# Attention scores with the head matrix folded into 33 key features instead of into the queries, and 3 of 16 probability tiles multiplied by the values in fp32

## What is computed

```python
c_q = h_t @ W_DQ + b_DQ                      # 32 query latents a token
c_kv = h_t @ W_DKV + b_DKV                   # 32 key/value latents a token
q_c, k_c, v_c = c_q @ W_UQ + b_UQ, c_kv @ W_UK + b_UK, c_kv @ W_UV + b_UV   # 8 heads of 128
q_r = c_q @ W_QR + b_QR                      # 8 heads of 32
k_r = h_t @ W_KR + b_KR                      # 32, the same for all heads
scores = einsum('bhsd,bhtd->bhst', concat(q_c, q_r), concat(k_c, k_r)) * scale
o = einsum('bhst,bhtd->bhsd', softmax(scores), v_c)
```

## Time and profile before

| | us |
|---|---|
| median of three runs | 1004.38 |
| profiled execution | 1002.61 |
| its span, first to last instruction | 1000.9 |
| first stage | 0 to 86 |
| attention, from its first PE instruction | 86 to 604 |
| the two later stages | 605 to 1000.9 |

### The profile page before, as it was taken

The page is one execution under the profiler, slowest core; times in us unless marked ns, Lnnn a source line. Parts: engine busy times, 40 slices in busy tenths (PEclk is TensorE's granted clock), DMA queues, the critical chain, the costliest instruction groups (busy, mean ns, idle before and its releaser), DMA issues. The chain is left out here.

```text
span 1000.9 us, 21467 instructions
## 1 busy us (share of the span) xinstructions
PE 881.8 (88%) x8406; PEld 527.7 (53%) x8406; DVE 713.9 (71%) x1315; ACT 588.0 (59%) x1004; POOL 655.7 (66%) x437
## 2 busy tenths in 40 slices
PE   4893899999999999999999988962499999999995
PEld 1350244444444444444444547862266777677764
DVE  4768888888888888888898836872075666566643
ACT  3750577777777777777777663664265446544650
POOL 4200599999999999999999993698404524442452
PEclk9995799999999999999999998985599999999998
DMA  9910000000000000000000004259525434543110
GB/s 279 339 43 0 1 2 2 2 2 2 2 2 2 2 2 2 2 2 2 2 2 1 3 1 169 99 198 320 201 69 162 143 107 140 175 142 123 43 52 19
DMA packets 48166, 71.61 MB, mean 72 GB/s; under 512 B 7508, under 2 KB 40473, under 8 KB 47938
## 3 DMA queue, kind: packets, MB, share of 16 engines
q1 hardware_dynamic: 38114, 53.13, 16.1%
q0 software_dynamic: 7680, 16.87, 5.2%
q10 hardware_dynamic: 2272, 0.24, 0.2%
HBM read 46.76 MB, written 29.67 MB: 76 GB/s over the span
## 5 line engine op out<-in xcount | busy, mean ns | idle before, releaser
L834 POOL TENSOR_TENSOR prob_lo<-prob 128x1024 f16<-128x1024 f32 x208 | 437.3, 2130 | 95.0 <-ACT prob L799 94.9
L799 ACT ACTIVATE prob<-st_ps 128x512 f32<-128x512 f32 x512 | 301.4, 597 | 131.8 <-PE st_ps L723 129.5
L859 DVE TENSOR_REDUCE part_max<-x_ps 128x1 f32<-128x512 f32 x512 | 325.1, 678 | 66.7 <-PE x_ps L733 65.7
L722 PE MATMUL st_ps<-QA,KA 128*128 128x512 f16 x512 | 198.1, 387 | 0.5 <-ACT prob L799 0.5
L723 PE MATMUL st_ps<-QB,KB 65*128 65x512 f16 x512 | 196.4, 384 | 0.0
L771 PE MATMUL acc_ps<-VV,prob 128*128 128x65 f16 x2048 | 159.3, 194 | 3.9 <-POOL prob_lo L834 3.9
L771 PEld LDWEIGHTS acc_ps<-VV,prob 128*128 128x128 bf16 x2048 | 143.6, 98 | 33.4 <-POOL prob_lo L834 6.1
L771 PE MATMUL acc_ps<-VV,prob_lo 128*128 128x65 f16 x2048 | 158.7, 194 | 0.0
L771 PEld LDWEIGHTS acc_ps<-VV,prob_lo 128*128 128x128 f16 x2048 | 134.9, 98 | 29.9
L1340 POOL DMA_INDIRECT out<-yo,xb x48 | 47.7, 993 | 153.3 <-DVE yo L1447 151.1
L732 PE MATMUL x_ps<-KA,QA 64*128 64x512 f16 x256 | 102.2, 399 | 20.8 <-DVE part_max L859 20.7
(11 more groups left out here) (177 smaller groups left out, 1346.7 us busy)
## 6 DMA issues: line engine op xcount, KB each, us to landing
w1f<-in_L_ffn_w SPq DMA_DIRECT2D x8, 1024.0 KB, 6.1
w2f<-in_L_ffn_w SPq DMA_DIRECT2D x8, 1024.0 KB, 6.1
xbuf<-zeros SPq DMA_DIRECT2D x7, 910.0 KB, 16.7
xb<-xbuf SPq DMA_DIRECT2D x8, 780.0 KB, 5.4
x<-in_L_attn_h_t SPq DMA_DIRECT2D x8, 512.0 KB, 8.9
out<-x SPq DMA_DIRECT2D x4, 1024.0 KB, 5.9
tbuf<-x SPq DMA_DIRECT2D x4, 1024.0 KB, 9.7
tbuf<-gb_row SPq DMA_DIRECT2D x4, 1024.0 KB, 4.7
```

The source lines that it names most:

```text
L722: mm(st_ps[i % 2][:], KA[:, at], QA[:, n % QRING, half], start=True, stop=False)
L799: nc.scalar.activation(prob[:, k, f * HALF:(f + 1) * HALF], st_ps[i % 2][:], ACT.Exp).then_inc(exp_done, 1)
L834: nc.gpsimd.tensor_tensor(prob_lo[:, k, :], prob[:, k, :], prob_top[:, k, :], ALU.subtract).then_inc(sub_pool, 1)
L859: nc.vector.tensor_reduce(part_max[:, n % 2, item // 2, item % 2:item % 2 + 1], x_ps[i % 3][:], AX.X, ALU.max).then_inc(smax_done, 1)
```

## The change

1. **The matrix goes into the keys.** `keys(n, f)` makes, from KA and a copy KB of its high rows, 98 rows of key features (33 numbers high, 32 and 33 more for the low parts) with two products, GH (128 rows) and GL (64 rows). ACT copies all 98 rows to KX, a ring of three heads; DVE then replaces rows 64 to 96 by the low part (`keys_low`). CQ is used as it is by all heads; it is there twice (parity of the head), for the sake of one row more, the maximum's. The second copy is made by a DMA at the start of the stage.
2. **A score half is one product** of 99 rows, KX against CQ.
3. **Maxima by 512 columns.** For every 128 queries there are two products of 98 rows, CQ against one half of KX; each is issued by itself when one of three x_ps buffers is free, one behind each score half. The 128 queries of a product are every eighth one, so mz lies in such an order that a DMA can write it into the row of CQ directly: `max_rows` on PE and ACT falls away. Before the first maxima product of a head PE waits for both halves of `keys_low` (kl_done).
4. **Whole tiles.** Tiles 1 and 6 of even heads and tile 3 of odd ones aren't split: PE multiplies prob (fp32) with V32, the values in fp32, 33 columns, 8 products a tile. DVE subtracts no tile any more; POOL subtracts 13 of 16 as before.
5. In the first stage, KC is no longer made, V32 is made by DVE (one addition a batch), and the folded matrix is made in two steps of four heads (`FOLD`) in place of one.

```diff
-        def maxima_of(p, k):
...
+                def scores(n, k, f):
...
+                    if k == 0 and f == 0:
                         te.wait_ge(mrow_in[n % 2], 16 * (n // 2 + 1))
-                    mm(st_ps[i % 2][:], KA[:, at], QA[:, n % QRING, half], start=True, stop=False)
-                    mm(st_ps[i % 2][:], KB[:, at], QB[:, n % QRING, half], start=False, stop=True).then_inc(scores_ready, 1)
+                    mm(st_ps[i % 2][:], KX[:, n % KRING, k * P:(k + 1) * P],
+                       CQ[:, n % 2, b * S + f * HALF:b * S + (f + 1) * HALF], start=True, stop=True).then_inc(scores_ready, 1)
...
-                    mm(x_ps[i % 3][:], QA[0:LR, n % QRING, at], KA[0:LR, b * S:b * S + HALF], start=True, stop=True)
-                    mm(x_ps[(i + 1) % 3][:], QA[LR:P, n % QRING, at], KC[LR:P, b, :], start=True, stop=True).then_inc(smax_ready, 1)
+                def maxima(n, j, f):
+                    i = (n * ST + j) * 2 + f
+                    if i >= 3:
+                        te.wait_ge(smax_done, i - 2)
+                    if j == 0 and f == 0:
+                        te.wait_ge(kl_done, 2 * n + 2)
+                        if n == 1:
+                            te.wait_ge(copied, 16)
+                    mm(x_ps[i % 3][:], queries_of[:, n % 2, b * P:(b + 1) * P, j],
+                       KX[0:QROWS, n % KRING, f * HALF:(f + 1) * HALF], start=True, stop=True).then_inc(smax_ready, 1)
...
+                def keys(n, f):
+                    if 2 * n + f:
+                        te.wait_ge(kl_done, 2 * n + f)
+                    mm(side_ps[0:QROWS, :], GH[:, h, :], KA[:, at], start=True, stop=False)
+                    mm(side_ps[0:QROWS, :], GL[:, h, :], KB[:, at], start=False, stop=True).then_inc(k_ready, 1)
...
+                    if k in whole(n):
+                        te.wait_ge(exp_done, (n * ST + k) * 2 + 2)
+                        for q in range(ST):
+                            last = mm(acc_ps[:, q, DC:VC], prob[:, k, q * P:(q + 1) * P], V32[:, b * ST + k, :],
+                                      start=False, stop=False)
...
+                def keys_low(n, f):
+                    v.wait_ge(kh_done, 2 * n + f + 1)
+                    at = KX[LR:QROWS - 1, n % KRING, f * HALF:(f + 1) * HALF]
+                    nc.vector.tensor_tensor(at, side_ps[LR:QROWS - 1, :], at, ALU.subtract).then_inc(kl_done, 1)
...
+                    if is_head(p + 2):
+                        maxima(p + 2, k, 1)
+                        if k == ST - 1:
+                            whole_rows(p + 2)
+                    if k - 1 in KEY_SLOTS and is_head(p + 3):
+                        keys_low(p + 3, KEY_SLOTS.index(k - 1))
```

More of the change, by code:

```diff
@@ L142, in adaln_block @@
         ukvT = sb(one, "ukvT", [P, H, 2 * DC])
-        G = sb(one, "G", [QROWS, H, P])
+        G = sb(one, "G", [P, H, QROWS])
         zeros = sb(one, "zeros", [P, 7, ROW])
@@ L344, in _ @@
                 pool.wait_ge(ln_rstd, 2)
-                fill(13, CQ[3 * DC:QROWS, :], 1.0)
+                fill(13, CQ[3 * DC:QROWS, 0, :], 1.0)
                 pool.wait_ge(const_p, 14)
-                for g in range(2, NG):
+                power(2)
+                pool.wait_ge(ln_rstd, 3)
+                fill(14, V32[:, :, DC:DC + 1], 1.0)
+                pool.wait_ge(const_p, 15)
+                for g in range(3, NG):
                     power(g)
@@ L498, in _ @@
                 queries_low(2)
-                side_out(GQS)
+                side_out(FOLD)
+                side_out(FOLD + 1)
                 take_values(2)
@@ L572, in side @@
                                                        ident[0:2 * DC, 0:2 * DC])
-                    elif n == GQS:
-                        for h in range(H):
-                            last = mm(bank[0:QROWS, h * DC:(h + 1) * DC], uqT[:, h, 0:QROWS], ukvT[:, h, 0:DC], start=True, stop=True)
+                    elif n >= FOLD:
+                        for i in range(4):
+                            h = 4 * (n - FOLD) + i
+                            at = slice(i * P, i * P + QROWS)
+                            for r in (0, LR):
+                                mm(bank[r:r + DC, at], ukvT[:, h, 0:DC], uqT[:, h, 0:QROWS], start=True, stop=True)
+                                last = mm(bank[r + DC:r + LR, at], qr[:, h, :], ident[0:QROWS, 0:QROWS], start=True, stop=True)
                     elif n < BIAS:
@@ L615, in _ @@
                 latent(2, 1)
-                side(GQS)
+                side(FOLD)
                 turn(7)
+                side(FOLD + 1)
                 values(2)
@@ L663, in adaln_block, with whole @@
         AHEAD = 4
-        QUERY_SLOTS = (4, 6)
-        FIRST_MAX = 0
-        ROW_SLOT = 1
-        def by_vector(n):
-            return (5, 7) if n % 2 else (5,)
+        KEY_SLOTS = (4, 6)
+        queries_of = CQ[0:QROWS, :, :].rearrange("c r (g t) -> c r g t", t=ST)
+        def whole(n):
+            return (3,) if n % 2 else (1, 6)
         def by_pool(n):
-            return [k for k in range(ST) if k not in by_vector(n)]
+            return [k for k in range(ST) if k not in whole(n)]
         pool_before = [sum(len(by_pool(m)) for m in range(n)) for n in range(HEADS)]
-        vector_before = [sum(len(by_vector(m)) for m in range(n)) for n in range(HEADS)]
         def slots():
@@ L784, in _ @@
                             values(p, k)
-                        if f == 0 and is_head(nm):
-                            maxima(nm, items[0] // 2)
-                    if k in QUERY_SLOTS and is_head(p + 3):
-                        query(p + 3, QUERY_SLOTS.index(k))
+                        if is_head(p + 2):
+                            maxima(p + 2, k, f)
+                    if k in KEY_SLOTS and is_head(p + 3):
+                        keys(p + 3, KEY_SLOTS.index(k))
                     if k < ST - 1 and is_head(p):
@@ L822, in _ @@
                             exponential(n, kk, f)
-                        if f == 0 and k == ROW_SLOT and is_head(p + 1):
-                            max_rows(p + 1)
                         if f == 0 and k == ST - 1 and is_head(p):
                             out_of_psum(p)
-                    if k in QUERY_SLOTS and is_head(p + 3):
-                        query(p + 3, QUERY_SLOTS.index(k))
+                    if k in KEY_SLOTS and is_head(p + 3):
+                        keys(p + 3, KEY_SLOTS.index(k))
             @block.gpsimd
```

177 lines of the change are left out of this document (60 added, 117 removed).

## The result

The changed kernel takes **1081.78 us** (median of four runs, 1075.08 to 1094.98) against 1003.13 before (four runs): the ratio is 1.076, with an interval of 1.070 to 1.082. It is slower by 79 us. Medians take in all executions but for g2_best_split_dve, whose 1024 us is of two of four, and ratios leave out those in a slower state with a lower mean clock (1094.98 us here, 1042 and 1045 in g2_best_split_dve). The forecast was 1054, with 1082 as the upper end of its range: the direction and the mechanism were right, the size was 28 us short, and the result lies inside the range by 0.2 us only.

A forecast was written before the change was run, and what follows sets the result against it. PE was taken as the bound, with POOL close behind. Heads +30, the rest -1 and clock +21 made +50 on a 1000.9 us span, 1051; offsets of 1.7 and 1.8 gave 1054 us, range 1018 to 1082.

The forecast's parts named there:

- The stall: Before each head's first maxima product, PE waits for DVE's low part of the keys: 2.14 us a head, plus or minus 0.3.
- The second wait: In slot 6, the keys' second half waits for the first half's low part: 0.4 us a head (0 to 0.5).
- heads and ramp: Attention: +30 us over the 30 heads with a later head's maxima beside them, +2 (0 to 5) at its start.
- PE's work alone: Products and weight loads on PE without waits: 13.87 us a head, against 14.8 before.
- The rival with four weight loads: Each fp32 whole-tile product loads weights four times, 0.43 us a product: +77 us, about 1130; chance 0.02.
- The exposed loads beside 64 rows: Unhidden weight loads around the keys' 64-row GL product: 0.1 us on each side, 0.4 a head (0 to 0.4).
- POOL: POOL's subtractions, with DVE's gone, take about 1.86 us each, 12.7 a head, so POOL isn't the bound.
- The rest: Outside the main heads: first stage 0 (-1 to +2), last two heads -3 us (-6 to 0).
- The clock: In the attention, the granted clock falls behind 16 of 30 stalls at 1.3 us each: +21 us.
- The rival that had the clock staying down: The clock falls at every stall, or stays down longer: +45 us, 1078 or more; chance 0.09.
- The rival on the other side: DVE's low part is ready before PE wants it, so no stall: 14.3 us a head, 970 us; chance 0.09.

The follow-up runs named there:

- g2_best_split_dve: Changed kernel with keys in slots 3 and 5, 128-row second key product, low part before reductions, and whole tiles split again, DVE subtracting three of 16: 1024 us.
- e1: Changed kernel with the key features made in slots 3 and 5 in place of 4 and 6: 993.29 us, ratio 0.989.
- f1: e1 with the second product of the key features over 128 rows in place of 64: 976.37 us, ratio 0.972.
- e3: Changed kernel with all 16 tiles split again, DVE subtracting three of them as before: 1110.81 us, ratio 1.106.
- g1: Changed kernel with only DVE's low part of the keys moved ahead of the reductions of slots 5 and 7: 976.03 us, ratio 0.971.
- e2: Changed kernel with eight unread products of 512 columns put before the wait for the low part: 1065.51 us, ratio 1.061.
- e4: Kernel before the change, with a head's first maxima product also waiting for DVE's low part of the second query half: 1055.85 us, ratio 1.051.
- f4: e2 with the second whole tile of even heads moved from 6 to 3: 1047.74 us, ratio 1.044.

## Why the prediction was right, and where it was short

**The stall: right in place, cause and number.** It was to be a row of L732 behind DVE's KX, once a head, of about 2 us; it is 27 times 2.25 us of idle time. Counted as the forecast counted it, from start to start, the stall is 2.43 us for 2.14, within the 0.3 allowed. The product was put at t + 3.71 from the start of slot 7 and came at t + 4.05. Of the 0.34, 0.03 are at the start (the reduction begins at t + 1.16 for 1.13), 0.24 in DVE's chain: `both` starts 0.72 us behind the reduction where the earlier trace rows have 0.61, and the low part 0.20 behind mz where they have 0.09. 0.02 are the low part's own 0.69 for 0.67, and 0.05 its way to PE. The step that was off is the assumption that the chain takes what it took before because the instructions have the same shapes. The low part now changes KX in place; whether that is the reason it starts later was not tried.

**The second wait: right in kind, too small.** Slot 6 was to take 2.27 us (0.4 of waiting) and took 2.54 (405.47 to 408.01). PE stands 0.47 between the end of the maxima's 0.22 us and L740, and then come 0.35 for the one product with 128 rows. Together the two steps, 0.40 in slots 7 and 0 and 0.27 in slot 6, make the usual pair of heads 16.44 and 17.77, 17.1 on average, for the 16.4 of the forecast. That is 0.7 us a head; heads and ramp were to cost 32 us and cost 50.

**PE's work alone: right.** A slot of two scores, two maxima and a split tile takes 1.36 us (forecast 1.344), a whole tile 1.71 (1.72), slot 4 with the keys 2.03 (1.98). There are 16 records to a whole tile, two a product. The rival with four weight loads (1130) is out: the Trainium skill's four passes of "FP8 and Floating Point Precision", section TensorE Precision Notes, may be inside, but the trace shows no more than 0.107 us for each of two records a product. The exposed loads beside 64 rows, booked at 0.4 us a head, cost about 0.5 (e1 against f1: 17 us over 32 heads).

**POOL: right.** All 174 subtractions from 140 to 620 us take 1.89 or 1.90 us; the long ones of the earlier trace rows went with DVE's. What I missed is the other half of this: I read the earlier trace rows as POOL's price for a collision, and not that DVE could be the one to pay. It made no difference to this forecast, but it is what the expectations of e3 and g2 missed.

**The rest: right.** The start of the program cost 1.4 us (forecast 0, between -1 and 2), the end gave 2.8 back (forecast 3).

**The clock: right in kind, wrong in both factors.** I had 16 falls at 1.3 us, from one fall of 3.3 us in the first stage. There are 8. Three short ones (3.4 us) cost 1.6 each, near to what I took. Three of 10.2 us cost 4.9 each, and the two in the distance from 158.0, of 13.7 and 3.4 us, 7.0 together. The last 5.7 us are no fall behind a stall, but the low clock from before the attention, which lasted 17 us longer. 32 us in all, for 21: half the falls at two and a half times the price (26.5 us for 8), so that two errors partly cancelled. The step that failed is the price: one example was taken for the size of all. A reading failed too: the clock was not at full speed through the whole attention before, as the 5 and the 7 in the earlier trace rows show. Nor is it so that no wait under 2 us cost any of it there: in the last head before, a wait of 1.31 us ends at 595.8, and a fall of 6.8 us begins there. The rival that had the clock staying down gave 1078, which is nearer to the result than the forecast was, though for another reason: its 45 us were thirty short falls.

The sum on the span was 32 (heads and ramp), 21 (clock), 0 and -3 (the ends): 50. That it holds within the stated range owes something to luck, since 1081.78 is 0.2 us under its end. It came out as 50, 32, 1.4 and -2.8: 81, of which 18 of the 31 us too few are the heads' and 11 the clock's. That the median is only 28 above the forecast is because it lies 1.6 under the profiled execution, where before it lay 1.8 above.

**The rival on the other side.** "The stall costs nothing" had 970 us, and the condition was put as the low part being taken before `both` and the reductions. The changed kernel doesn't do that, so the case didn't come. g1 is that case made by hand, and gives 976. That this is so near to 970 is in part luck. The 970 had 0.4 us a head for the second wait, which g1 doesn't have; its heads take 14.6 us where the sum of PE's work alone was 13.87. In the 0.7 between them PE waits, each time under 0.5 us, for ACT's exponentials and DVE's reductions, waits that the forecast let go because the stall would cover them. The 106 us between g1 and after are the price of the order alone.

**What stays open.** Why one fall lasts 3.4 us and another 10, and why many stalls of 2.27 us bring none, the runs don't say; e2, e4 and f4 show only where falls begin and that they go when the stall is filled and the whole tile of slot 6 is moved. Nor did a run have the changed kernel's stall and order with the clock held up and nothing else; f4 is the nearest.

## What to carry to other kernels

When a wait is put on another engine's result, count from a common start when that engine's queue reaches the instruction, with all that stands in front of it, and when the result is wanted. Here it was an instruction of 0.69 us behind 2.05 us of others, ready over 2 us after it was wanted, and moving it ahead of them (with its twin in slot 5) was worth a tenth of the whole time. Before a change is given up as slower, look whether the loss sits in such a place: the idea was 2.9% faster with it mended, and 6% with three more small changes (the key slots, the rows of the second product, one whole tile a head). And look where instructions with two SBUF inputs on DVE and POOL meet: here PE was the cheaper place for such a tile even at three and a half times its own price.

## What the hardware showed that I had not expected

- DVE's subtraction 128x1024 (fp32 in, fp16 out) takes 1.22 us if POOL's of the same size starts with it (POOL then 2.96), and 2.5 to 2.8 us if POOL's began 0.1 to 0.5 us before (POOL then 1.9). Alone they take 1.21 and 1.89: who comes first isn't slowed down.
- The granted clock fell to half, for 3.4 us in most cases and up to 13.7, after stalls of 1.7 to 2.3 us in otherwise dense work: in every fourth head in e4 (stalls of 1.70 us), at 7 of some 30 stalls in the changed kernel, about once a head in e3. Eight useless products of 512 columns in the stall did not hold it up (e2) until a whole tile in fp32, 16 records with 33 columns each, was moved away from the next wait of 0.31 us too (f4).
- A product with 64 rows between those with 98 to 128 costs 0.1 us on each side; filling it with rows of zeros (and reading KA in place of KB) gave 17 us in 32 heads, for no more time of its own.
- The weights of the maxima are every eighth column of CQ, and their products still start 0.22 us behind the score before them: such a stride costs nothing that can be seen here.
